# A two-layer attention and expert kernel: fewer blank rows, weights loaded in pieces, one accumulator at the end

## The reference

```python
xn = _layernorm(x)
x = x + _L0_attn_ref(xn, ...) + _L0_ffn_ref(xn, ...)   # linear attention; 32 experts, 8 of them per token, plus shared
xn = _layernorm(x)
x = x + _L1_attn_ref(xn, ...) + _L1_ffn_ref(xn, ...)   # gated recurrence; 8 experts, 2 of them per token, plus shared
# an expert, for the tokens that chose it, weighted by cw:
h = silu(xn @ wg.T) * (xn @ wu.T)                      # inner width 176
acc = acc + cw[:, None] * (h @ wd.T)
```

## Time and profile before

| | us |
|---|---|
| three runs | 1078.21, 1078.83, 1081.71 |
| median | 1078.83 |
| the profiled execution | 1076.17 |
| its span, first to last instruction | 1074.4 |

### The profile page before, as it was taken

The page is one execution under the profiler, slowest core; times in us unless marked ns, Lnnn a source line. Parts: engine busy times, 40 slices in busy tenths (PEclk is TensorE's granted clock), DMA queues, the critical chain, the costliest instruction groups (busy, mean ns, idle before and its releaser), DMA issues.

```text
span 1074.4 us, 15432 instructions
## 1 busy us (share of the span) xinstructions
PE 840.0 (78%) x3786; PEld 594.7 (55%) x3786; DVE 353.4 (33%) x1040; ACT 315.9 (29%) x847; POOL 494.9 (46%) x383
## 2 busy tenths in 40 slices
PE   3889979600269999999999999461198999999980
PEld 2647746500146666666666666240086666777760
DVE  3642266500012332333323332111515163344343
ACT  4321211100123333333333333120241123345440
POOL 3002767766226666666666666232323714333330
PEclk9999999955679999999999999775559999999995
DMA  9999996432779989998988988966701324443339
GB/s 319 311 308 341 395 329 201 161 114 105 276 218 184 186 185 189 183 185 185 188 187 181 187 186 186 272 148 137 199 1 46 110 88 75 73 65 63 38 49 218
DMA packets 130978, 189.91 MB, mean 177 GB/s; under 512 B 12752, under 2 KB 107344, under 8 KB 129912
## 3 DMA queue, kind: packets, MB, share of 16 engines
q1 hardware_dynamic: 94704, 139.28, 43.0%
q0 software_dynamic: 36192, 49.65, 27.2%
HBM read 94.49 MB, written 94.39 MB: 176 GB/s over the span
## 4 chain that ended last, share of the span: by engine, by line
PE 58%; POOL 12%; DMA 9%; SPq 8%; issue 8%; DVE 2%; ACT 1%; POOLq 0%; DVEq 0%; ACTq 0%
PE banks L825 21%; PE banks L851 16%; POOL xg L527 12%; SPq L416 5%; PE banks L810 4%; PE banks L836 4%; DMA xg<-zrow 3%; SPq L424 3%; DMA xb<-xg 2%; PE banks L668 2%; PE banks L650 2%; PE banks L641 1%; PE banks L898 1%; DMA wd<-in_wdn 1%; DMA accs<-yb,xb 1%
## 5 line engine op out<-in xcount | busy, mean ns | idle before, releaser
L536 POOL DMA_INDIRECT accs<-yb,xb x198 | 310.4, 1567 | 341.2 <-ACT yb L1107 328.8
L825 PE MATMUL banks<-wgu,xt 128*128 x636 | 235.7, 467 | 0.3 <-ACT xt L1095 0.3
L527 POOL DMA_INDIRECT xg<-tok,slot_int x160 | 157.4, 984 | 154.6 <-issue 64.7
L851 PE MATMUL banks<-wd,ht 88*128 88x256 f32 x636 | 186.0, 386 | 42.6 <-issue 21.0
L1482 DVE SCALAR_TENSOR_TENSOR hid<-sg,xb,banks 128x176 f32<-128x176 f32 x198 | 78.6, 397 | 424.2 <-ACT sg L1101 405.5
L810 PE MATMUL banks<-cst,xb 128*128 128x128 f32 x396 | 108.5, 276 | 86.1 <-DMA xb<-xg 85.0
L1095 ACT COPY xt<-banks 128x256 f32<-128x256 f32 x198 | 73.8, 373 | 316.6 <-PE banks L810 316.6
L851 PEld LDWEIGHTS banks<-wd,ht 88*128 88x128 f32 x636 | 98.4, 195 | 83.9 <-issue 66.3
L810 PEld LDWEIGHTS banks<-cst,xb 128*128 128x128 f32 x396 | 56.3, 143 | 129.4 <-DMA xb<-xg 86.9
L825 PEld LDWEIGHTS banks<-wgu,xt 128*128 128x128 f32 x636 | 98.1, 194 | 41.3 <-issue 26.7
L1107 ACT COPY yb<-banks 128x256 f32<-128x256 f32 x198 | 73.7, 372 | 129.7 <-PE banks L851 129.7
(11 more groups left out here) (204 smaller groups left out, 865.0 us busy)
## 6 DMA issues: line engine op xcount, KB each, us to landing
xb<-xg SPq DMA_DIRECT2D x198, 144.5 KB, 3.4
wd<-in_wdn SPq DMA_DIRECT2D x159, 176.0 KB
xg<-zrow SPq DMA_DIRECT2D x3, 3901.5 KB, 35.4
xg<-zrow SPq DMA_DIRECT2D x3, 3757.0 KB, 33.5
accs<-zeros SPq DMA_DIRECT2D x20, 544.0 KB, 20.6
xg<-zrow SPq DMA_DIRECT2D x1, 5635.5 KB, 44.1
wgu<-in_wgu SPq DMA_DIRECT2D x2, 2816.0 KB, 21.7
wgu<-in_wgu SPq DMA_DIRECT2D x1, 4224.0 KB, 23.8
```

Source lines behind the costliest of these rows:

```text
L527: pool.indirect_dma_start(xg[n], bass.IndirectOffsetOnAxis(ap=(slot_int1 if n else slot_int)[:, t, k:k + 1], axis=0), tokw[:, t, :], None)\
L536: pool.indirect_dma_start(accs[a], bass.IndirectOffsetOnAxis(ap=xb[:, g % RING, ROW_ID:ROW].bitcast(U32), axis=0), yb[:, g % YB_RING, :], ...
L825: mm = pe.matmul(bank[2 + g % 2][:, 0:2 * F0], xt[:, g % 2, k, :], w[:, bass.ds(expert[g], 1), k, :].rearrange("p a n -> p (a n)"), start= ...
L851: mm = pe.matmul(bank[7][:, 0:D], ht[:, g % 2, c, :], w, start=c == 0, stop=c == 1, skip_group_check=True)
```

## The change

- **Blanking.** The tile `zrow` becomes `blank_rows`: 8 rows in each of 128 partitions, so that 16 partitions hold the blanks of a block. SyncE stores blanks only into blocks 128 to 158 of layer 0 (which may stay empty) in 4 DMAs, and into all 39 blocks of layer 1 in 5. Each expert's last block in layer 0 is blanked by four indirect DMAs on GpSimd, 128 x 9248 B each, whose targets VectorE works out from the block ends in `place`. GpSimd waits for them before the scatter.
- **Bulk loads.** The 24 later experts go in six DMAs of four experts: one behind all 12 first block rows, the others at blocks 0, 4, 8, 12 and 16. Layer 1's shared weights go at block 40, `og` at 43, `kq` at 46, into space that the attention has left; `gu1` and `dn1` go behind the last block. Accumulators 0 and 1 are loaded in eight pieces of four DMAs at blocks 148 to 155, and VectorE sums each quarter between blocks.
- **Accumulators.** The last 14 blocks of layer 0 (before 8) use accumulators 2 and 3. In layer 1 blocks 0 to 11 alternate, blocks 12 to 28 use the first, the last ten the second. The first is loaded whole as soon as it is closed, the second in quarters at the end.
- **Norm of layer 1.** ScalarE takes the next group's square root before it applies a group, and copies the turned tokens out one group later.

The DVE operations of `place`, the layout changes and the core of the rest:

```diff
+FULL = T * TOPK0 // P
+CHUNK = 8
+CHUNKS = P // CHUNK
+BLANK_STORES = -(-(NB0 - FULL) * CHUNKS // P), -(-NB1 * CHUNKS // P)
+ENDS = E0 * CHUNKS // P
-ACCS0, LAST0, ACCS1 = 4, 8, 2
+ACCS0, LAST0 = 4, 14
+ACCS1, BOTH1, LAST1 = 2, 12, 10
+ACC_OF += [ACCS0 + (b % ACCS1 if b < BOTH1 else int(b >= NB1 - LAST1)) for b in range(NB1)]
-W_CHUNKS = ((0, W_EARLY), (W_EARLY, 12), (12, 20), (20, E0))
+W_CHUNKS = ((0, W_EARLY),) + tuple((low, low + 4) for low in range(W_EARLY, E0, 4))
+SHARED1_AT = 40
+CLOSED_AT = NB0 - LAST0 + 3
...
+            def blank_blocks(n, low, high):
+                for at in range(low * CHUNKS, high * CHUNKS, P):
+                    many = min(P, high * CHUNKS - at)
+                    sp.dma_start(chunks_of(n)[at:at + many, :], blank_rows[0:many].rearrange("p r w -> p (r w)"))\
+                        .then_inc(xg_blank[n], 16)
...
-            sp.wait_ge(ids_made, 1)
-            fill_rows(0, FILLS0)
+            sp.wait_ge(ids_made, 2)
+            blank_blocks(0, FULL, NB0)
...
-                if g == 2:
-                    for c in range(1, len(W_CHUNKS)):
-                        experts_in(c)
+            experts_in(1)
...
+                if g % 4 == 0 and 2 + g // 4 < len(W_CHUNKS):
+                    experts_in(2 + g // 4)
-                if g == DEAD_AT:
-                    sp.wait_ge(gu_mm, DEAD_AT)
+                if g == SHARED1_AT:
                     sp.dma_start(shw1[:], sh_gu1).then_inc(shared_in[1], 16)
                     sp.dma_start(shd1[:], sh_dn1).then_inc(shared_in[1], 16)
-                    sp.dma_start(gu1[:], wgu1).then_inc(gu1_in, 16)
-                    sp.dma_start(dn1[:], wdn1).then_inc(gu1_in, 16)
+                if g == SHARED1_AT + 3:
                     sp.dma_start(og[:], w_og).then_inc(og_in, 16)
-                if g == CLOSED_AT:
-                    sp.wait_ge(acc_st, 16 * BATCH)
-                    for a, dst in ((0, acc), (1, tok)):
+                if g == SHARED1_AT + 6:
+                    sp.dma_start(kq[:], w_kq).then_inc(kq_in, 16)
+                if 0 <= g - CLOSED_AT < 2 * NBLK:
+                    q, a = divmod(g - CLOSED_AT, 2)
+                    if q == 0:
                         sp.wait_ge(added_to[a], 16 * adds_to(a))
-                        rows_by_chunk(dst, accs[a], slice(0, NT), sums_early)
+                    rows_by_chunk(tok if a else acc, accs[a], slice(4 * q, 4 * q + 4), sums_early[q])
...
-            sp.dma_start(kq[:], w_kq).then_inc(kq_in, 16)
+            sp.wait_ge(gu_mm, NB0)
+            sp.dma_start(gu1[:], wgu1).then_inc(gu1_in, 16)
+            sp.dma_start(dn1[:], wdn1).then_inc(gu1_in, 16)
...
-            for a in range(ACCS0, ACCS0 + ACCS1):
-                sp.wait_ge(added_to[a], 16 * adds_to(a))
-            for h in range(2):
-                for a, dst in ((ACCS0, fin_a), (ACCS0 + 1, fin_b)):
-                    rows_by_chunk(dst, accs[a], slice(HT * h, HT * h + HT), fin_in[h])
+            sp.wait_ge(added_to[ACCS0], 16 * adds_to(ACCS0))
+            rows_by_chunk(fin_a, accs[ACCS0], slice(0, NT), fin_early)
+            sp.wait_ge(added_to[ACCS0 + 1], 16 * adds_to(ACCS0 + 1))
+            for q in range(NBLK):
+                rows_by_chunk(fin_b, accs[ACCS0 + 1], slice(4 * q, 4 * q + 4), fin_in[q])
...
+            pool.wait_ge(xg_blank[0], 16 * BLANK_STORES[0])
+            pool.wait_ge(ends_found, 1)
+            for i in range(ENDS):
+                pool.indirect_dma_start(chunks_of(0), bass.IndirectOffsetOnAxis(ap=blank_idx[:, i:i + 1], axis=0),
+                                        blank_rows[:].rearrange("p r w -> p (r w)"), None).then_inc(ends_blank, 16)
+            pool.wait_ge(ends_blank, 16 * ENDS)
...
+            norm_std(NBLK)
             for c in range(NBLK, 2 * NBLK):
-                norm_std(c)
+                if c + 1 < 2 * NBLK:
+                    norm_std(c + 1)
                 norm_apply(c)
-                width_out(c)
+                if c > NBLK:
+                    width_out(c - 1)
+            width_out(2 * NBLK - 1)
...
+                if n == 0:
+                    sel = cst[:, C_SEL:C_SEL + P // CHUNKS].unsqueeze(1).to_broadcast([P, ENDS, P // CHUNKS])
+                    link(v.tensor_tensor(end_of[:], end[:].rearrange("p (i g) -> p i g", i=ENDS), sel, ALU.mult))
+                    link(v.tensor_reduce(end_sum[:], end_of[:], AX_X, ALU.add))
+                    v.tensor_scalar(blank_idx[:], end_sum[:], float(CHUNKS), cst[:, C_SUB:C_SUB + 1], ALU.mult, ALU.add)\
+                        .then_inc(ends_found, 1)
...
-                if g == SUM_AT:
-                    dve.wait_ge(sums_early, 16 * 2 * BATCH)
+                q, odd = divmod(g - CLOSED_AT - 4, 2)
+                if 0 <= q < NBLK and not odd:
+                    dve.wait_ge(sums_early[q], 16 * 2 * BATCH)
+                    tiles = slice(4 * q, 4 * q + 4)
+                    link(v.tensor_tensor(acc[:, tiles], acc[:, tiles], tok[:, tiles], ALU.add))
...
+            dve.wait_ge(fin_early, 16 * BATCH)
             for q in range(NBLK):
                 tiles = slice(4 * q, 4 * q + 4)
-                if q % 2 == 0:
-                    dve.wait_ge(fin_in[q // 2], 16 * 2 * BATCH)
-                link(v.tensor_tensor(acc[:, tiles], acc[:, tiles], fin_a[:, tiles], ALU.add))
+                last = v.tensor_tensor(acc[:, tiles], acc[:, tiles], fin_a[:, tiles], ALU.add)
+            link(last)
+            for q in range(NBLK):
+                tiles = slice(4 * q, 4 * q + 4)
+                dve.wait_ge(fin_in[q], 16 * BATCH)
                 v.tensor_tensor(acc[:, tiles], acc[:, tiles], fin_b[:, tiles], ALU.add).then_inc(fin_added, 1)
```

109 lines of the change are left out of this document (53 added, 56 removed).

## The result

| | before | changed |
|---|---|---|
| median, us | 1079.26 (4 runs) | 1029.44 (4 runs, 1027.64 to 1039.11) |
| ratio | | 0.9557, 95% interval 0.9495 to 0.9619 |
| profiled execution, us | 1076.17 | 1039.11 |
| its span, us | 1074.4 | 1037.3 |

The account below looks back on a forecast made before the run. TensorE's matmuls set the block pace, 2.50 us, and waits made holes around it; 7.4 + 4.8 + 17.1 + 30.4 + 1 + 10.5 = 71.2 us off the 1074.4 span gave 1003.2, on the runs' median 1007; range 988 to 1030.

Parts of the forecast that it names:

- Scatter start, length, first blocks: Before layer 0's first add: gains of 7.4 us (scatter call at 90), 4.8 (shorter scatter), 17.1 (no stand for block rows).
- the rival with dearer calls: Blanking: a 9248 B row costs GpSimd eight times a 1156 B one, blanks done no earlier; 1019 us, chance 0.10.
- Pieces among the blocks: Layer 0's block loop: weight pieces delay the down weights behind them by only 2 us in all (0 to 9).
- The cover of 6.4: Layer 0's loop: down weights, asked for three blocks ahead, have 6.4 us; behind a piece they land after an estimated 5.6.
- The rival: Layer 0's loop: the pieces still stall the blocks, 34 us instead of 2; 1039 us, chance 0.10.
- The tail of layer 0: Last 14 blocks of layer 0: adds to two accumulators wait for landings, beside quarter loads; cost 12.4 us (4.8 to 20).
- Norm of layer 1: Between the layers: ScalarE's root ahead and late copy-out, until TensorE's logits become the limit; gain 1 us (0 to 3).
- Layer 1's end: Layer 1's last adds and final sums: 13.9 us saved, less 3.4 for a later last landing; gain 10.5 (6 to 13).
- Two landings fit into a pair: Layer 1's adds on one accumulator: landing 3.8 us, pair of adds 8.4, so the chain keeps up except at the end.
- one accumulator at a loaded landing in all of layer 1: Layer 1: 26 gaps become landings of 8.7 us, 120 us instead of 3.4; slower than before, 1123 us, chance 0.03.
- Quarter loads that don't overlap: Layer 0's loop: quarter loads run one after another, 109 us instead of 20; about 1080 us, no change, chance 0.01.
- The slow landing for all 14 blocks: Layer 0's last 14 blocks: two accumulators at the loaded landing throughout, 28 us instead of 12.4; 1023 us, chance 0.12.

## Why the prediction came out as it did

- **Scatter start, length, first blocks** (29.3 forecast, 29.7 measured): right, part by part. The first scatter call was forecast at 90 and came at 89.9, and the two queues did share about evenly while both had work (0.40 and 0.32 MB from 74 to 76 us), though in the prediction's own sum the blanks served last would have come at 90.8, so this time says little about the share; blanks with rows of 9248 B take GpSimd 0.96 to 1.15 us a call, no more than the 1156 B rows did, so the rival with dearer calls fell.
- **Pieces among the blocks**: the step that failed. The term was 2 us (0 to 9). In the profiled execution it was 18.3 in the first 22 blocks, and, since blocks 40 to 60 with layer 1's pieces took 53.1 us instead of 49.9, another 3.2 (49.9 to 58.5 us in other profiles); in the mean of the ten profiles with these pieces it was 14.3 and 5.5. I had worked out a landing of 5.6 us for the small weights behind a piece from 3.6 us of transfer at 396 GB/s, a rate that was read where the queue had the engines nearly to itself. In the loop the blocks' own traffic keeps them busy at 0.9; there a piece landed after 9.3 us, and the down weights behind it were used 8.5 to 9.2 us after their request. The cover of 6.4 was 2 to 3 us short, which is the size of the stalls (2.2 to 3.2). This is the sign of being wrong that the prediction named: TensorE waits for down weights behind the pieces. The rival had the mechanism, not the price: 34 us at 3.5 a MB. That its 1039 is the time of the profiled execution is chance, since the pieces make up less than two thirds of what is missing.
- **The tail of layer 0** (12.4 forecast): the right size for a reason that is at most half right, and so in part luck. Adds 128 to 158 took 86.8 us, 11.8 above 30 x 2.50 = 75.0. The price was put on landings at two accumulators; but without the quarter loads and their sums two accumulators cost nothing (32.3 us for 13 steps), and with them four cost nearly the same (40.9). Landings did grow beside the loads, to 7.8 us. What the traces show holding TensorE is the item that had no price of its own: VectorE's waits for the quarters, 8.9 us in all, and TensorE's for `ht` behind them.
- **Norm of layer 1** (gain 1): not there. This stretch went from 139.3 to 144.2 us in the profiled execution and to 138.9 in the best other one. Before has one profile here, so up to 2 or 3 us may be the scatter of executions. The last of the late sums starts 0.7 to 2.6 us later after the landing than before, in all profiles that leave this stretch alone; why is open.
- **Layer 1's end** (10.5 forecast, 0.8 measured): the term "last landing 3.4 later" (2 to 5) was too small; the loop grew by 10.8. "Two landings fit into a pair" left out the time from a landing to the next add, about 0.7 us (the tail's term had an estimated 0.3): 4.45 an add and 8.9 a pair instead of 8.4. That cost 2 to 3 us up to block 28 and 3.6 in the last ten. And the 2 MB load beside them was counted as a small disturbance, where it held one add for 9.7 us and cost 5 to 8. The tail itself came as forecast: 17.4 us after the last landing against 15.6.
- **The rivals**: one accumulator at a loaded landing in all of layer 1 didn't come; it came for one add. Quarter loads that don't overlap are excluded: the last 13 steps took 43.2 us in all, not 109. The slow landing for all 14 blocks didn't come either: the tail cost 11.8 us, not 28.

So the direction was right, and the range too narrow at the top: two of the three prices of moved loads took the load as if little else went on beside it, and both erred to the same side, while the width was made as if they were independent.

## What to carry to other kernels

Size a bulk load that runs beside a tight loop by the lead of the smallest transfer behind it, not by bandwidth: 352 KB pieces cost a fifth of what 1408 KB pieces did, at the same bytes. Take the landing times for such a sum from a stretch in which the DMA engines are as busy as they will be. A wait for a load that is put on an engine which every block passes through, as VectorE's for the quarters, stops the blocks behind it. Before saving a load at the end, price what an accumulate chain on one target and that load do to the adds beside it; here they took back all that the end had gained.
